# Weight casts split over two engines, sigmoids through a buffer of their own, FFN weights loaded one block ahead

## The reference, cut to what matters

```python
xn = _ln(x, ln1_g, ln1_b); xp = _shift(xn)
k = (xn * mix_k + xp * (1.0 - mix_k)) @ Wk          # v with mix_v, Wv
r = jax.nn.sigmoid((xn * mix_r + xp * (1.0 - mix_r)) @ Wr)
wkv = _wkv(k, v, time_decay, time_first)            # a = ew*a + e^k*v, b = ew*b + e^k, a/b
x = x + r * wkv @ Wo
yn = _ln(x, ln2_g, ln2_b); yp = _shift(yn)
kk = jnp.square(jax.nn.relu((0.5 * yn + 0.5 * yp) @ Wfk))
rr = jax.nn.sigmoid(yn @ Wfr)
x1 = _layernorm(x_in + (x + rr * (kk @ Wfv)))       # first half of the layer
y = jax.nn.silu(_ln(x1) @ dequant(fc1) + fc1_bias)
z = y @ dequant(fc2) + fc2_bias
out = _layernorm(x1 + (x1 + 0.5 * z))
```

## Time and profile before

| what | us |
|---|---|
| median of the 2 runs | 4667.17 |
| lowest and highest run | 4522.76, 4811.57 |
| the profiled execution, its own time | 4528.21 |
| its span, core 5, the slowest | 4526.6 |
| spans of the 8 cores | 4475.9 to 4526.6 |
| TensorE busy in that span | 2985.8 (66%) |
| VectorE, ScalarE, GpSimd busy | 1462.8, 1109.2, 167.3 |

### The profile page before, as it was taken

How to read it: one execution, slowest core, us unless ns; L and a number is a source line. 1 busy time by engine, 2 the same in 40 slices (tenths; PEclk the granted TensorE clock), 3 DMA queues, 4 the chain that set the end, 5 groups by cost and what they waited for, 6 DMA issues and landing times.

```text
span 4526.6 us, 40922 instructions; the slowest of 8 cores (4475.9 to 4526.6 us)
## 1 busy us (share of the span) xinstructions
PE 2985.8 (66%) x11840; PEld 1207.0 (27%) x11840; DVE 1462.8 (32%) x2819; ACT 1109.2 (25%) x1694; POOL 167.3 (4%) x292
## 2 busy tenths in 40 slices
PE   1122189969568765877486847695587658774866
PEld 0000022224223322333132313232233223331422
DVE  4021232431541154214622263215411542136121
ACT  2231132222231313221232123122313132212221
POOL 2112201200000000000000000000000000000000
PEclk9565566679779887989798968897898879896988
DMA  6655445534224331434132422343243314341333
GB/s 154 187 175 163 159 144 182 187 110 124 102 77 121 108 104 57 133 102 138 54 117 86 135 75 93 92 124 102 77 122 106 105 60 129 96 144 54 107 93 110
DMA packets 260842, 521.07 MB, mean 115 GB/s; under 512 B 26081, under 2 KB 81633, under 8 KB 250386
## 3 DMA queue, kind: packets, MB, share of 16 engines
q1 hardware_dynamic: 178096, 387.52, 27.6%
q0 software_dynamic: 24192, 79.28, 5.2%
q10 hardware_dynamic: 58338, 51.66, 4.1%
HBM read 457.54 MB, written 60.82 MB: 115 GB/s over the span
## 4 chain that ended last, share of the span: by engine, by line
PE 43%; DMA 22%; DVE 18%; ACT 8%; issue 7%; POOL 1%; ACTq 1%; DVEq 1%; SPq 0%; POOLq 0%
PE psO L802 14%; PE psA L834 9%; PE psB L834 8%; DMA fvb<-s_w 4%; DMA fvb<-s_fv 3%; DVE stB_sum L497 2%; DMA s_fv<-stb 2%; PE psO L613 2%; DVE bigbf L580 2%; DMA stf<-L_attn_Wfk 2%; PE psA L434 2%; DVE sc_aa L661 2%; DVE sc_bb L571 2%; PE psB L434 2%; DVE sc_bb L672 2%
## 5 line engine op out<-in xcount | busy, mean ns | idle before, releaser
L802 PE MATMUL psO<-fvb,bigbf 128*128 128x512 bf16 x4096 | 1072.7, 397 | 217.8 <-DMA fvb<-s_w 68.4
L802 PEld LDWEIGHTS psO<-fvb,bigbf 128*128 128x128 bf16 x4096 | 392.5, 100 | 842.3 <-issue 460.1
L834 PE MATMUL psB<-TB,fkb 128*128 128x512 bf16 x2048 | 515.0, 397 | 42.5 <-DMA fkb<-s_fk 37.0
L613 PE MATMUL psO<-bigbf,wsm 128*128 128x512 bf16 x1024 | 295.5, 453 | 364.0 <-ACT bigbf L702 229.8
L834 PE MATMUL psA<-TB,fkb 128*128 128x512 bf16 x2048 | 508.9, 393 | 13.5 <-DMA fkb<-s_fk 7.7
L860 DVE TENSOR_TENSOR bigbf<-bigbf 128x512 bf16<-128x512 bf16 x256 | 108.4, 425 | 697.5 <-ACT bigbf L856 697.5
L927 DVE SCALAR_TENSOR_TENSOR T<-Q,psO 128x512 f32<-128x512 f32 x64 | 44.0, 688 | 852.6 <-PE psO L920 846.9
L544 PE MATMUL psT<-ident_sb,ztm 128*128 128x128 bf16 x512 | 69.5, 292 | 344.0 <-DVE ztm L523 204.6
L613 PE MATMUL psA<-bigbf,wsm 128*128 128x512 bf16 x256 | 102.8, 535 | 288.1 <-DVE sc_ekv L650 82.7
L834 PEld LDWEIGHTS psB<-TB,fkb 128*128 128x128 bf16 x2048 | 204.3, 102 | 322.3 <-issue 123.2
L506 ACT ACTIVATE zt<-T,stB_nm 128x1024 bf16<-128x1024 f32 x64 | 73.6, 1151 | 847.4 <-DVE stB_m L503 847.4
(11 more groups left out here) (136 smaller groups left out, 2989.4 us busy)
## 6 DMA issues: line engine op xcount, KB each, us to landing
fkb<-s_fk SPq DMA_DIRECT2D x256, 256.0 KB, 2.9
fvb<-s_fv SPq DMA_DIRECT2D x256, 256.0 KB, 2.8
fkb<-s_w SPq DMA_DIRECT2D x256, 256.0 KB, 2.8
fvb<-s_w SPq DMA_DIRECT2D x256, 256.0 KB, 2.8
stq<-L_ffn_fc_q ACTq DMA_DIRECT2D x128, 256.0 KB, 4.6
x<-xcore SPq DMA_DIRECT2D x8, 2048.0 KB, 8.7
wsm<-s_wk SPq DMA_DIRECT2D x16, 1024.0 KB, 7.0
wsm<-s_wv SPq DMA_DIRECT2D x16, 1024.0 KB, 9.0
```

The lines of the kernel that those rows point to most:

```text
L613: E("tensor", lambda e, mo=mo, k=k, ps=ps, wt=wt: e.matmul(ps[:], wt[:, 1024 * (k % 4) + 128 * mo:1024 * (k % 4) + 128 * (mo + 1)], bigbf[ ...
L802: E("tensor", lambda e, mm=mm, j=j, mpar=mpar, sl=sl: e.matmul(psO[j][:], bigbf[:, 512 * mm + 128 * j:512 * mm + 128 * (j + 1)], fvb[:, 10 ...
L834: E("tensor", lambda e, m=m, k=k, ps=ps, par=par: e.matmul(ps[:], fkb[:, 1024 * par + 128 * k:1024 * par + 128 * (k + 1)], TB[:, 512 * k:5 ...
```

## The change

Three edits. `pump_pair` is called without arguments at the top level and in the k stage, so the second cast of each of these 24 pairs is VectorE's; the v stage keeps both on ScalarE. In the r stage the sigmoid writes a new bf16 buffer `rsg` of 512 columns, the gate reads it and writes bigbf, and both are emitted after the matmuls of the next tile; in half 0 the sigmoid of tile mo now stands behind the casts pumped in tile mo, where it stood ahead of them. In `ffn_pair` the load of fkb for block m + 1 is emitted at block m, ahead of fvb, with the first one ahead of the loop.

```diff
+        rsg = T("rsg", [128, 512], BF16)
...
-                    pump_pair("scalar", "scalar")
-                    pump_pair("scalar", "scalar")
+                    pump_pair()
+                    pump_pair()
...
+            sig_fns = []
             for mo in range(KT):
                 ps, psn = kvr_mm(hh, mo, wsm[1], "wsm1", wsm[2], "wsm2", 16,
                                  f"{hh}_rmm", pool=RPS)
-                E("scalar", lambda e, mo=mo, ps=ps: e.activation(
-                    out=bigbf[:, 512 * (24 + mo):512 * (25 + mo)], in_=ps[:],
-                    func=AF.Sigmoid),
-                  reads=[psn], writes=[bbuf(24 + mo)], tag=f"{hh}_sg{mo}")
-                E("vector", lambda e, mo=mo: e.tensor_tensor(
-                    out=bigbf[:, 512 * (24 + mo):512 * (25 + mo)],
-                    in0=bigbf[:, 512 * (24 + mo):512 * (25 + mo)],
-                    in1=T2[:, 512 * mo:512 * (mo + 1)], op=OP.mult),
-                  reads=[bbuf(24 + mo), "T2"], writes=[bbuf(24 + mo)],
-                  tag=f"{hh}_gt{mo}")
+
+                def mkf(mo=mo, ps=ps, psn=psn):
+                    E("scalar", lambda e: e.activation(
+                        out=rsg[:], in_=ps[:], func=AF.Sigmoid),
+                      reads=[psn], writes=["rsg"], tag=f"{hh}_sg{mo}")
+                    E("vector", lambda e: e.tensor_tensor(
+                        out=bigbf[:, 512 * (24 + mo):512 * (25 + mo)],
+                        in0=rsg[:], in1=T2[:, 512 * mo:512 * (mo + 1)],
+                        op=OP.mult),
+                      reads=["rsg", "T2"], writes=[bbuf(24 + mo)],
+                      tag=f"{hh}_gt{mo}")
+                sig_fns.append(mkf)
+                if mo > 0:
+                    sig_fns[mo - 1]()
                 if h == 0:
                     pump_pair()
                     pump_pair()
+            sig_fns[KT - 1]()
...
+                if cho == 0:
+                    E("q_sync", lambda e: e.dma_start(
+                        out=fkb[:, 0:1024], in_=scr_blk[0, :, 0:1024]),
...
-                    if cho == 0:
-                        E("q_sync", lambda e, m=m, par=par: e.dma_start(
-                            out=fkb[:, 1024 * par:1024 * (par + 1)],
+                    if cho == 0 and m + 1 < FT:
+                        mp, pp = m + 1, (m + 1) % 2
+                        E("q_sync", lambda e, mp=mp, pp=pp: e.dma_start(
+                            out=fkb[:, 1024 * pp:1024 * (pp + 1)],
...
-        pump_pair("scalar", "scalar")
-        pump_pair("scalar", "scalar")
+        pump_pair()
+        pump_pair()
         stage_pre(0)
...
```

More of the change, by code:

```diff
@@ L813, in ffn_pair @@
                 pend = []
+                if cho == 0:
+                    E("q_sync", lambda e: e.dma_start(
+                        out=fkb[:, 0:1024], in_=scr_blk[0, :, 0:1024]),
+                      reads=[blkn + "@0", blkn + "@1"],
+                      writes=["fkb0"], tag=f"{tagp}b0")
                 for m in range(FT):
@@ L816, in ffn_pair @@
                     sl = (m // 2) % 2
-                    if cho == 0:
-                        E("q_sync", lambda e, m=m, par=par: e.dma_start(
-                            out=fkb[:, 1024 * par:1024 * (par + 1)],
-                            in_=scr_blk[m // 2, :,
-                                        1024 * (m % 2):1024 * (m % 2 + 1)]),
+                    if cho == 0 and m + 1 < FT:
+                        mp, pp = m + 1, (m + 1) % 2
+                        E("q_sync", lambda e, mp=mp, pp=pp: e.dma_start(
+                            out=fkb[:, 1024 * pp:1024 * (pp + 1)],
+                            in_=scr_blk[mp // 2, :,
+                                        1024 * (mp % 2):1024 * (mp % 2 + 1)]),
                           reads=[blkn + "@0", blkn + "@1"],
-                          writes=[f"fkb{par}"], tag=f"{tagp}b{m}")
+                          writes=[f"fkb{pp}"], tag=f"{tagp}b{mp}")
                     if par == 0:
```

## The result

| what | us |
|---|---|
| changed kernel, median of 12 runs (lowest to highest) | 4578.39 (4545.98 to 4842.84) |
| kernel before, median of 11 runs (lowest to highest) | 4522.76 (4517.01 to 4811.57) |
| ratio | 1.0081, 95% interval 1.0050 to 1.0112 |

The change makes the kernel 0.8% slower, 37 us: real by its interval, and within the 2% that counts as no change. On the level of 4522.76 us the changed kernel stands at 4522.76 x 1.0081 = 4559 us.

The account below looks back on a forecast made before the run. No engine was taken as the bound throughout; the change was priced in half 0's weight casts and every half's FFN sweep. 15 + 2 + 13 - 4 = +26 us on 4528.21 us gave 4554 us, range 4495 to 4605 us.

Parts of the forecast that it names:

- I forecast on the level of the profiled one: Whole kernel: the sum is added to the profiled execution's 4528.21 us, not to the median of 4667.17 us.
- the sentence that +0.6% can't be told from no change: Whole kernel: +0.6% is under what a measurement can tell from no change, about 2% or 90 us.
- The first rival: Ring and FFN sweep: fewer ring casts, x0 stalls and short fkb waits gone, mixes hidden, 4451 us; chance 8%.
- Part A: Half 0's weight casts: 24 go to VectorE; waiting behind the mixing costs 22 us, alternation gains 7, +15 us.
- The rival that the ring catches up: Half 0's cast ring: it catches up after mix_vr, moved casts cost about 0, 4539 us; chance 17%.
- The port: GpSimd's DMA issues in half 0: each moved VectorE cast holds the shared port, 4570 us; chance 5%.
- the 17 us: GpSimd's DMA issues: by the skill's rule each moved cast could hold POOL its full length, 24 x 0.69 us.
- The forecast's 1.4 us: GpSimd's DMA issues: by the profile row the moved casts hold POOL only 24 x 0.06 us; taken inside the rounding.
- Part B: r stage: later sigmoid and gate through rsg cost 0 in halves 1 to 7 and +2 us in half 0.
- Part C: FFN sweep: fkb one block ahead makes x0 leave 2.2 us later, six times, +13 us; short waits -4.
- "-4" for the short waits: FFN sweep: fvb no longer right ahead of odd blocks takes some short fkb waits, -4 us, bounds 0 and -24.
- The third rival: FFN sweep's odd blocks: fkb and fvb leave close together, fkb lands later, 112 us more, 4666 us; chance 7%.

Follow-up runs that it names:

- A: Kernel before with only the 24 casts moved to VectorE (8 pairs at the top, 16 in the k stage), against before: mean core +20 us [15, 26].
- B: Kernel before with only rsg and the sigmoid and gate one tile later, against before: ratio 1.0002 [0.9982, 1.0021].
- C: Kernel before with only fkb loaded one block ahead on SP's queue, against before: ratio 1.0040 [1.0011, 1.0069].
- A late: Kernel before with second casts on VectorE only in the k stage from tile 1 on (14 pairs), against before: ratio 0.9987 [0.9960, 1.0013].
- x0 first: Kernel before with fkb one block ahead, but x0's load put ahead of fkb block 5, against before: ratio 0.9979 [0.9954, 1.0003].

## Why the prediction was right, and where it was not

**The whole.** The forecast was +26 us on the level of the profiled execution, 4554 us; measured is +37 us [23, 51] by the ratio, 4559 us on that level, and +26 [21, 29] by the mean core. The step that failed is the one that made a time of the sum: "I forecast on the level of the profiled one". The 26 us were added to one execution's 4528.21 us, while the time given for the kernel before was 4667.17. Beside that, 4554 is 2.4% faster, and the change is 0.8% slower. Of 11 runs the median before is 4522.76 and that of the changed kernel 4578.39; only the ratio of runs made side by side says which way the change goes. With it falls the sentence that +0.6% can't be told from no change: the interval of the ratio is 0.3% to either side. By the ratio the sum itself is also 11 us short, within the interval. The two profiles lie below both measures: their slowest cores are 19.8 us apart (4546.4 and 4526.6), the means over their cores 22.4 (4520.8 and 4498.4).

By the mean core the sum is right and its terms are less so: A +20 [15, 26] for 15, B -1 [-4, 2] for 2, C +6 [3, 8] for 9, the one whose interval leaves the forecast out. That they come to 25 and not to 35 or 15 is in part luck. The first rival, that the change gains what it looks like, falls with the signs of A and C.

**Part A, +15: right step by step.** Predicted and found (core 6): mixing for k begins at 82.4, found 80.40; cast 13 ends at 101.0, found 98.9; the mixing for v and r begins at 107.8, found 107.93, and ends at 144.2, found 144.7; cast 17 ends at 144.9, found 145.4. That mixing for k was 2 us ahead of the forecast changed nothing behind it, since cast 15 then stood 8.43 us idle for its load. Over the stretch A costs 15 to 17 us. Cast 17 ends 22.6 us later than the 122.81 of the kernel before, where 22 was taken for the wait behind the mixing, and "A late" shows the other half: 0.3 to 0.5 us a pair, where 0.45 was taken. The rival that the ring catches up falls: the loss stays outside the range of the same code at every line of the table.

**The port: its mechanism is real, its price is not.** GpSimd's timeline and DVE's, after, core 6:

```profile
191.47 0.54 POOL L354 DMA_DIRECT2D s_wo<-stb  x1 [4.93 <-DMA s_wo<-stb]
...
233.12 1.02 POOL L354 DMA_DIRECT2D s_wfr<-stb  x1 [6.41 <-ACT T L633]
```
```profile
191.18 0.69 DVE L349 CAST stb<-stf 128x1024 bf16<-128x1024 f32 x1 [5.72 <-DMA s_wo<-stb]
...
233.33 0.69 DVE L349 CAST stb<-stf 128x1024 bf16<-128x1024 f32 x1 [9.94 <-DMA stf<-L_attn_Wfr]
```
The issue at 191.47 took its usual 0.54 us: the cast was already 0.29 us old and over in time. The one at 233.12, with a cast 0.21 us behind its start, took 1.02 and ended 0.12 after the cast. That is no chance. In the profiles of the kernel before, the changed one (the one shown here) and the other nine versions, all cores, 110 GpSimd DMA issues have a cast of DVE starting between 0.24 us before and 0.23 us behind their own start, and every one of them ends 0.12 or 0.13 us after that cast, having taken up to 1.04 us. With a cast that starts 0.24 us behind the issue or later, the issue takes 0.54 or 0.55 even with the whole cast inside or beside it. So the cast does hold the issue, to its own end, when it comes in the issue's first 0.2 us. The Trainium skill ("SBUF — State Buffer", SBUF: two separate sides) says that GpSimd can't write a DMA's descriptors while a VectorE copy in a two-port mode holds the port pair that they share; this trace agrees that there is such a hold. Which mode the cast ran in it doesn't show.

What fails is the 17 us, which had every moved cast meet an issue at its start. With A alone 3.1 issues a core do (means over cores), 0.7 us longer in all; in the changed kernel 3.2, 0.9 us. GpSimd's 232 issues of writes out of stb (of the casts and of the dequantisation) take 127.9 us with A alone, 127.8 in the changed kernel and 127.5 before. The forecast's 1.4 us came near this by luck: in the row that it took, the cast had 0.07 us left when the issue began, which couldn't show the hold.

**Part B, +2: right within its bounds, by another way than given.** The wait at the end of the r stage was thought to grow; it moved from the output projection to the r matmuls and the sum stayed.

**Part C, +9: the right mechanism, two terms mis-sized.** "The removed stall is paid back in full, and 2.2 us more, six times: +13". Found: the stop comes back one block later (block 6, 4.84 us a half) instead of within the square's, as the prediction's own list of signs had it, and the square's grows by 2.98. In all a half stops 2.7 us longer (15.1 against 12.4), not 2.2: 16 us for the 13. "-4" for the short waits is about right: the waits ahead of mm1 fell by 5.8, 1.6 of it at x0. Together the FFN waits grew by 12.4 us, the halves 1 to 7 by 1.7 each, 12 us, which is no more than the same code differs by (475.4 to 477.3 us a half). Half 0 gets shorter instead (below), which the forecast didn't have. The mean core shows +6 [3, 8] for both, the ratio +18 [5, 31]. The forecast's account had 9.

**The third rival**, that odd blocks pay for fkb beside fvb, would have shown in fkb's landing (2.9 before, 2.8 with C alone, 3.0 after) and in waits at the odd blocks (psB). Neither is there: psB's waits for fkb fell from 40.5 us to 10.7 (by form, above).

**Left open.** With C alone half 0 gets shorter: from the last pair of Wfr sigmoids to the write of its output, the stretch with the dequantisation, it lasts 571.2 us, and 571.6 with x0 first (medians over cores). The kernel before has 579.2, and A, A late and B, with the same code there, 578.9, 576.8 and 576.1: 5 to 8 us, though the changed kernel has 575.1. 4.6 us of it are idle time of TensorE ahead of the dequantisation's sums (27.5 against 32.1; 30.0 to 30.6 in the other three); the rest wasn't traced. It is also open why the ratio, of slowest cores, gives C three times what the mean core gives; their intervals meet.

## What to carry to other kernels

A cast given to an idle-looking engine is also put into that engine's row: look at what stands ahead of it there, not at its busy share, and give it over only from the point where that row is free. The place of a large load on a queue counts: one block later for x0 made its consumer 3 us late. Where the consumer blocks an in-order engine, issue the load many blocks early and cut the consumer into pieces that fit that engine's gaps. Of all that was tried, this alone paid more than 1%, and it was found by asking what ends the stall that comes after the removed one.

## What was not expected of the hardware

- A stop of 4.4 us is followed by a granted clock of 0.50 (1.2 GHz) for the next 3.6 us: the stop costs 1.7 us beyond itself. Removing the stops at x0 went with 18.2 us less of TensorE's busy time, without a matmul less.
- A cast on VectorE from float32 to bf16, 0.69 us long, holds a GpSimd DMA issue until 0.12 us after the cast's end if it starts in the issue's first 0.2 us (or runs already with some 0.45 us to go), and not at all if it starts later. Over the 44 casts of the changed kernel that came to 0.9 us a core.
- A 2 MB load of x0 issued at block 0 took nothing visible from the sweep's own loads: the median landing of fkb is 2.8 us, where the kernel before has 2.9.
